# One VectorE product for the weighted one-hots of all parts or heads, and the attention product two sets later

## What is computed

```python
def spmm(x):
    msgs = edge_val[:, None] * x[edge_col]
    return jax.ops.segment_sum(msgs, edge_row, num_segments=n)
acc = cur = ebds
for _ in range(3):
    cur = spmm(cur)
    acc = acc + cur
x = _layernorm(x + acc)
...
h = (x @ W_node.T).reshape(num_nodes, 4, 32)
att = leaky(sum([h[src], h[tgt], e] * a, axis=-1))       # one number per edge and head
ex = exp(att - m[tgt])                                    # m: the target's maximum, at least 0
w = ex / denom[tgt]
h_prime = segment_sum(w[:, :, None] * h[src], tgt)
x = _layernorm(x + h_prime)
```

## Time and profile before

| | us |
|---|---|
| median of three runs | 1680.29 |
| profiled execution | 1682.1 |
| its span, first to last instruction | 1680.3 |
| setup, 0 to 84 | 84 |
| adjacency stage, 84 to 452 | 368 |
| three products with the matrix, 452 to 893 | 441 |
| scores, 893 to 1075 | 182 |
| attention stage, 1075 to 1650, and its end | 605 |

### The profile page before, as it was taken

How to read it: one execution, slowest core, us unless ns; L and a number is a source line. 1 busy time by engine, 2 the same in 40 slices (tenths; PEclk the granted TensorE clock), 3 DMA queues, 4 the chain that set the end, 5 groups by cost and what they waited for, 6 DMA issues and landing times.

```text
span 1680.3 us, 50213 instructions
## 1 busy us (share of the span) xinstructions
PE 1396.0 (83%) x22245; PEld 1008.0 (60%) x22245; DVE 1059.3 (63%) x2069; ACT 680.2 (40%) x1575; POOL 140.0 (8%) x102
## 2 busy tenths in 40 slices
PE   4969899986399999999997998567888886888885
PEld 4968789876344454454446888545555554555554
DVE  5499999999500010000116888788888887888873
ACT  3246565654200000001111000166766777677775
POOL 2611101110000000000000000111111011110000
PEclk9999898998799999999997999768888887788887
DMA  5628677755498879969972776200000000000000
GB/s 198 219 94 243 184 212 204 221 145 132 128 348 317 302 282 339 305 213 370 301 257 78 206 217 205 60 11 12 12 11 10 12 12 11 12 9 13 25 3 23
DMA packets 214644, 250.32 MB, mean 149 GB/s; under 512 B 43578, under 2 KB 146487, under 8 KB 214294
## 3 DMA queue, kind: packets, MB, share of 16 engines
q1 hardware_dynamic: 210422, 236.52, 43.6%
q0 software_dynamic: 4000, 10.54, 2.1%
HBM read 197.88 MB, written 49.14 MB: 147 GB/s over the span
## 4 chain that ended last, share of the span: by engine, by line
PE 47%; DVE 31%; DMA 6%; issue 5%; DVEq 4%; ACT 4%; SPq 1%; ACTq 1%; POOL 0%; POOLq 0%
PE bank L680 24%; PE bank L746 9%; PE bank L757 8%; DVE Hw L1163 8%; DVE L L1153 6%; DVE Hx L1346 5%; DVE Lq L1339 4%; DMA lob<-slp 2%; DVE sel L1278 2%; PE bank L717 2%; DMA drow<-in_dst,rowi 2%; DMA hib<-slp 2%; ACT Att L1009 1%; DVEq L1157 1%; DVE Hh L1155 1%
## 5 line engine op out<-in xcount | busy, mean ns | idle before, releaser
L1009 ACT COPY Att<-bank 128x400 f32<-128x400 f32 x800 | 334.9, 540 | 168.2 <-PE bank L746 167.5
L746 PE MATMUL bank<-Hx,Lq 64*128 64x100 f16 x6400 | 241.3, 223 | 88.9 <-DVE Hx L1346 83.3
L746 PEld LDWEIGHTS bank<-Hx,Lq 64*128 64x128 f16 x6400 | 176.6, 102 | 176.3 <-DVE Hx L1346 90.4
L757 PE MATMUL bank<-Att,xa 128*32 128x128 f32 x5000 | 243.0, 307 | 37.8 <-ACT oT L1016 37.8
L607 PE MATMUL bank<-L,Hw 128*52 128x128 bf16 x4800 | 178.1, 233 | 56.2 <-DVE Hw L1163 53.8
L1346 DVE TENSOR_TENSOR Hx<-Hq,wdup 128x832 f16<-128x832 f16 x400 | 205.3, 588 | 4.1 <-issue 0.4
L607 PEld LDWEIGHTS bank<-L,Hw 128*52 128x52 bf16 x4800 | 154.1, 113 | 65.4 <-DVE Hw L1163 58.7
L1163 DVE TENSOR_TENSOR Hw<-Hh,dup 64x832 bf16<-64x832 bf16 x300 | 176.0, 587 | 8.1 <-PE bank L607 1.1
L889 ACT COPY rows<-bank 116x512 f32<-116x512 f32 x200 | 117.2, 586 | 151.2 <-PE bank L607 142.4
L757 PEld LDWEIGHTS bank<-Att,xa 128*32 128x32 f32 x5000 | 123.8, 117 | 77.5 <-ACT Att L1009 41.6
L717 PE MATMUL bank<-Tp,lob 128*128 128x100 bf16 x2418 | 152.5, 210 | 15.6 <-DVE sel L1278 13.6
(11 more groups left out here) (174 smaller groups left out, 1362.8 us busy)
## 6 DMA issues: line engine op xcount, KB each, us to landing
pieces<-adj SPq DMA_DIRECT2D x90, 1280.0 KB, 8.9
adj<-rows SPq DMA_DIRECT2D x100, 416.0 KB
lob<-slp SPq DMA_DIRECT2D x26, 992.0 KB, 6.2
ea<-in_edge_attr SPq DMA_DIRECT2D x25, 992.0 KB, 8.1
hib<-slp SPq DMA_DIRECT2D x78, 64.0 KB, 4.8
pieces<-adj SPq DMA_DIRECT2D x15, 320.0 KB, 3.1
lh_d<-dup SPq DMA_DIRECT2D x25, 64.0 KB, 3.9
lhd<-lh_d SPq DMA_DIRECT2D x25, 64.0 KB, 1.8
```

What stands on the lines that cost most here:

```text
L746: m = pe.matmul(bank[i % 3 * 2 + d][:, v * H * NB:(v + 1) * H * NB].rearrange("p (h i) -> p h i", h=H), Lq[n % 2][rows, pp, :], Hx[n % 2][ ...
L757: m = pe.matmul(bank[7][h * HD:(h + 1) * HD, 0:P], xa[:, i, h * HD:(h + 1) * HD], Att[j % 2][:, h * NB + i, :], start=(i == 0), stop=(i == ...
L1009: m = act.copy(o[:, d, :, :], bank[i % 3 * 2 + d][:, 0:4 * H * NB].rearrange("p (q i) -> p i q", q=4))
```

## The change

The weights of a slot are laid beside each other, and one product covers them all.

- Adjacency: `dup` keeps the low and the high index; the three weight parts go into a new tile `dupw` in which a slot's parts stand beside each other. TensorE's `turn_records` writes them into the bank three words apart for that, and ScalarE's `duplicate` becomes two copies. `Hw` has the part inside the slot. `Hh` is made once for both halves, in the first. The six products become two, one for each half of the partitions, of 96 x 26 elements.
- Attention: the same with `wdup`, where a slot's four heads stand beside each other (`turn_weights` writes four words apart), with `Hq` made once for both halves, and with two products of 3328 elements instead of eight of 832.
- The attention product of the block before starts behind set 2 (`LATE`) and is spread over 14 sets instead of 16. The turn of the result comes behind set 1 instead of set 2. ScalarE copies `oT` ahead of set 0's evacuation instead of behind it.

```diff
+LATE = 2
...
-                Hw = [sb(f"Hw{i}", [P, 3, HP, 2, HIP], BF16, c) for i in range(2)]
-                Hh = sb("Hh", [P, 2, HP, HIP], BF16, c)
+                Hw = [sb(f"Hw{i}", [P, HP, 3, 2, HIP], BF16, c) for i in range(2)]
+                Hh = sb("Hh", [P, 2, U, HIP], BF16, c)
...
-                dup = sb("dup", [P, 3, 5, U, 2], BF16, c)
+                dup, dupw = sb("dup", [P, 3, 2, U, 2], BF16, c), sb("dupw", [P, 3, U, 3, 2], BF16, c)
...
-            wdup = sb("wdup", [P, 2, 2 * H, U, 2], F16, c)
+            wdup = sb("wdup", [P, 2, 2, U, H, 2], F16, c)
...
                 for q in range(5):
-                    m = pe.matmul(bank[2][:, q * U:(q + 1) * U], Z[:, j % 2, q, :], Jb[:, :], start=True, stop=True)
+                    o = bank[2][:, q * U:(q + 1) * U] if q < 2 else bank[2][:, 2 * U:5 * U].rearrange("p (u k) -> p u k", k=3)[:, :, q - 2]
+                    m = pe.matmul(o, Z[:, j % 2, q, :], Jb[:, :], start=True, stop=True)
...
                 for q in range(2 * H):
-                    m = pe.matmul(bank[6][:, q * U:(q + 1) * U], Z16[:, j % 2, q // H, q % H, :], J16[:, :], start=True, stop=True)
+                    m = pe.matmul(bank[6][:, :].rearrange("p (k u h) -> p k u h", k=2, h=H)[:, q // H, :, q % H],
+                                  Z16[:, j % 2, q // H, q % H, :], J16[:, :], start=True, stop=True)
...
-                        if 1 <= j <= NB:
-                            product(j - 1, q * NB // SETS, (q + 1) * NB // SETS)
-                        if q == 2 and j >= 2:
+                        if 1 <= j <= NB and q >= LATE:
+                            product(j - 1, (q - LATE) * NB // (SETS - LATE), (q - LATE + 1) * NB // (SETS - LATE))
+                        if q == 1 and j >= 2:
                             turn_result(j - 2)
...
                 act.copy(dup[:, j % 3, :, :, :].rearrange("p q u k -> p (q u) k"),
-                         bank[2][:, 0:5 * U].rearrange("p (n o) -> p n o", o=1).broadcast_to([P, 5 * U, 2])).then_inc(s["dup_sb"], 1)
+                         bank[2][:, 0:2 * U].rearrange("p (n o) -> p n o", o=1).broadcast_to([P, 2 * U, 2]))
+                act.copy(dupw[:, j % 3, :, :, :].rearrange("p u q k -> p (u q) k"),
+                         bank[2][:, 2 * U:5 * U].rearrange("p (n o) -> p n o", o=1).broadcast_to([P, 3 * U, 2])).then_inc(s["dup_sb"], 1)
...
+                        if q == 0 and j >= 2:
+                            result_evacuated(j - 2)
                         if j < NB:
                             weights_set(j, q)
-                        if q == 0 and j >= 2:
-                            result_evacuated(j - 2)
...
+            def beside(a, n):
+                return a.rearrange("p u (o n k) -> p u o n k", o=1, k=2).broadcast_to([a.shape[0], HP, n, HIP // 2, 2])
+            def inside(a):
+                return a.rearrange("p u q (o k) -> p u q o k", o=1).broadcast_to([a.shape[0], HP, a.shape[2], HIP // 2, 2])
...
-                dve.tensor_tensor(Hh[:, n % 2, :, :].rearrange("p u (n k) -> p u n k", k=2), pair_hi,
-                                  spread(dup[:, j % 3, 1, us, :], HIP // 2), ALU.is_equal)
+                if hf == 0:
+                    dve.tensor_tensor(Hh[:, j % 2, :, :].rearrange("p u (n k) -> p u n k", k=2), pair_hi, spread(dup[:, j % 3, 1, :, :], HIP // 2),
+                                      ALU.is_equal)
...
-                for k in range(3):
-                    for d in range(2):
-                        rows = slice(d * U, (d + 1) * U)
-                        m = dve.tensor_tensor(Hw[n % 2][rows, k, :, d, :].rearrange("p u (n k) -> p u n k", k=2),
-                                              Hh[rows, n % 2, :, :].rearrange("p u (n k) -> p u n k", k=2),
-                                              spread(dup[rows, j % 3, 2 + k, us, :], HIP // 2), ALU.mult)
+                for d in range(2):
+                    rows = slice(d * U, (d + 1) * U)
+                    m = dve.tensor_tensor(Hw[n % 2][rows, :, :, d, :].rearrange("p u q (n k) -> p u q n k", k=2),
+                                          beside(Hh[rows, j % 2, us, :], 3), inside(dupw[rows, j % 3, us, :, :]), ALU.mult)
...
-                dve.tensor_tensor(Hq[:, n % 2, :, :].rearrange("p u (n k) -> p u n k", k=2), pair_hi,
-                                  spread(lhd[:, j % 3, 1, us, :], HIP // 2), ALU.is_equal)
+                if hf == 0:
+                    dve.tensor_tensor(Hq[:, j % 2, :, :].rearrange("p u (n k) -> p u n k", k=2), pair_hi, spread(lhd[:, j % 3, 1, :, :], HIP // 2),
+                                      ALU.is_equal)
                 dve.drain()
                 for k in range(2):
-                    for h in range(H):
-                        m = dve.tensor_tensor(Hx[n % 2][:, k, :, h, :].rearrange("p u (n k) -> p u n k", k=2),
-                                              Hq[:, n % 2, :, :].rearrange("p u (n k) -> p u n k", k=2),
-                                              spread(wdup[:, j % 2, k * H + h, us, :], HIP // 2), ALU.mult)
+                    m = dve.tensor_tensor(Hx[n % 2][:, k, :, :, :].rearrange("p u h (n k) -> p u h n k", k=2),
+                                          beside(Hq[:, j % 2, us, :], H), inside(wdup[:, j % 2, k, us, :, :]), ALU.mult)
```

More of the change, by code:

```diff
@@ L167, in build @@
             Lq = [sb(f"Lq{i}", [P, HP, P], F16, c) for i in range(2)]
-            Hq = sb("Hq", [P, 2, HP, HIP], F16, c)
+            Hq = sb("Hq", [P, 2, U, HIP], F16, c)
             Hx = [sb(f"Hx{i}", [P, 2, HP, H, HIP], F16, c) for i in range(2)]
@@ L274, in store_dup @@
                 sp.wait_ge(s["dup_sb"], j + 1)
-                sp.dma_start(lh_d[j, :, :], dup[:, j % 3, 0:2, :, :].rearrange("p q u k -> p (q u k)")).then_inc(s[f"dup{j % 3}"], 16)
+                sp.dma_start(lh_d[j, :, :], dup[:, j % 3, :, :, :].rearrange("p q u k -> p (q u k)")).then_inc(s[f"dup{j % 3}"], 16)
             def adjacency():
@@ L607, in octet @@
                         mm = pe.matmul(bank[m % 2][c * U:c * U + 2 * HIP, v * P:(v + 1) * P],
-                                       Hw[n % 2][:, k, pp, :, :].rearrange("p d i -> p (d i)"), L[n % LB][:, pp, :],
+                                       Hw[n % 2][:, pp, k, :, :].rearrange("p d i -> p (d i)"), L[n % LB][:, pp, :],
                                        start=(k == 0), stop=(k == 2), tile_position=(0, c * U))
@@ L997, in duplicate_weights @@
                     act.wait_ge(s["hx_ready"], 2 * (j - 1))
-                act.copy(wdup[:, j % 2, :, :, :].rearrange("p q u k -> p (q u) k"),
+                act.copy(wdup[:, j % 2, :, :, :, :].rearrange("p q u h k -> p (q u h) k"),
                          bank[6][:, :].rearrange("p (n o) -> p n o", o=1).broadcast_to([P, BANK, 2])).then_inc(s["wdup_sb"], 1)
```

4 lines of the change are left out of this document (2 added, 2 removed).

## The result

The changed kernel takes 1602.3 us (median; 1599.3 to 1605.0), the kernel before 1680.1 in the same session. The ratio is 0.9538, with a 95% interval of 0.9523 to 0.9554: 78 us less, where 73 were forecast (1607, range 1588 to 1645). The profiled execution took 1605.0 us, its span is 1603.3. The total given for a kernel is the median of its runs, without one of experiment 8 that took 4137 us where the other three took 1605 to 1609.

The account below looks back on a forecast made before the run. VectorE was taken to bound the adjacency, and a loop through VectorE, TensorE and ScalarE the attention stage. 1682.1 - 31 (adjacency) - 42 (attention) = 1609 us, 1607 on the median's scale, range 1588 to 1645.

Parts of the forecast that it names:

- Price of the merged products: VectorE, both stages: 1.02 us for 1664 elements, 1.46 for 2496, 1.89 for 3328.
- the line: VectorE product time from products of 832 and 4096 elements: 0.522 ns an element plus 153 ns.
- The rival of one element at a time: VectorE, both stages: merged products stream at 1.044 ns an element, total near 1890 us; chance 0.06.
- the 3.5 us that I took off for TensorE: Adjacency: loss from TensorE's low-clock rounds reaching VectorE, taken from 34.5 us to leave 31 us gained.
- the low clock last from set 0 on to 5.8 us: Attention, TensorE: sets 0 to 4 and the turn of the result run slow, so set 8 starts at 9.31 us.
- TensorE late by a hair: Attention, set 8: TensorE arrives at 9.31 us, after VectorE's second-half Hx at 9.03.
- both changes are needed: Attention, set 8: with the old second half, Hx would come at 9.94 us instead of 9.03.
- the 1.76 us a round: Attention: gain from a round of 21.95 us to 20.19; 40 us in 23 rounds.
- The end of 53 us: Attention: largest gain, if TensorE is never slow and the round is VectorE's 19.18 + 0.73 us.
- Writes with a step: Turns writing into the bank 3 or 4 words apart: same time taken, 0.41 us for the weights' turn.
- the rival's price: Slow stepped writes in the turns: at double time, 0.41 us in each of 23 attention rounds, 9 us; chance 0.11.
- 1 us to the block behind the last `Lq`: Attention: gain for the last block, where one shorter half counts; part of the 42 us.

Follow-up runs that it names:

- experiment 8: Changed kernel with ScalarE's copy of oT put behind the evacuation of set 0 again, the product still starting at set 2: 1607.6 us, ratio 0.9568.
- experiment 1: Kernel before with only the adjacency part of the change (Hw in two products, Hh once a round, dupw, stepped records' turn): 1644.9 us, ratio 0.978.
- experiments 2 and 3: On the kernel before: first, only the merged products of attention, 1678.2 us; second, only the later attention product with oT copied earlier, 1662.4 us.
- Experiment 4: Changed kernel with both turns writing their columns densely again, so outputs aren't the reference's: 1604.6 us, ratio 0.954.
- experiments 9 and 10: Weights' turn and copy behind set 7, finish ahead of the odd half: on the kernel before, 1677.9 us; on the changed kernel without later product, 1640.6 us.

## Why the prediction was right, point by point

- **Price of the merged products.** 1889 and 1453 ns measured, 1.89 and 1.46 us worked out by the line; 1019 ns for 1664 elements, 1.02 worked out. The rival of one element at a time is out.
- **Adjacency.** The round is 12.75 us, 12.77 forecast. The term was mis-sized by the 3.5 us that I took off for TensorE: 34.3 us came in the trace (the first product with the matrix at 431.13, was 465.43) and 35.4 in experiment 1. VectorE waited 2.0 us for TensorE in the stage of after. The step that failed is the belief that the rounds at a low clock would come as before and hand half of their delay on. From `L` to `L`, 6 of 24 rounds of before stand at 0.74 to 0.84 (not 7, as I had counted), and of after 21 at 1.00 and three at 0.85 to 0.87. TensorE also waits less for `Hw` there, 27.4 us instead of 53.8; that this is why the clock stayed up isn't shown. And in experiment 1, where four rounds stood at 0.73 to 0.90, VectorE waited for TensorE only 3.1 us in the whole stage.
- **Attention.** 38.4 + 4.9 = 43.3 us, 42 forecast. The common round is 20.22, forecast 20.19, but by steps that miss in opposite directions. Set 8 starts at 9.09 us and not at 9.31: I had the low clock last from set 0 on to 5.8 us, with five slow sets. In the round shown it stands from 1.1 to 4.5 us behind set 0, with two sets and a part of one slow, so TensorE is ready at 8.40 and VectorE's `Hx`, at 9.03 as worked out, ends last. "TensorE late by a hair" was wrong, "both changes are needed" right (experiments 2 and 3). From set 8 to `Lq` are 4.07 us, not 3.87, and that is the turn.
- **Luck in the sum of the attention.** I took the 1.76 us a round from a round of 21.95 us, but the twelve rounds of the earlier trace rows last 22.19 in the mean. Two forms take turns in most of them: 22.00 us with set 0 at 1.2 GHz, the one that I read, and 22.43 with set 0 at 2.4 GHz. So the ordinary round fell by 2.0 us, and four long rounds gave some 5 us back; the two nearly cancel. The end of 53 us, too, comes out only from the mean of 22.19: 21.95 - 19.91 = 2.04 us in 23 rounds, and 2 us, are 49. Below stand set 0 of the round of before that I didn't read, and the `Lq` 22.43 us behind the last one in the earlier trace rows.

```profile
1295.47 0.54 PE L746 MATMUL bank<-Hx,Lq 64*128 64x100 f16 x16 [2.77 <-DVE Hx L1346]
```
```profile
1310.87 2.29 DVE L1339 TENSOR_TENSOR Lq<-iota_lo,lhd 128x4096 f16<-128x4096 bf16 x1 [2.31 <-PE bank L746]
```

- **Writes with a step.** I took no cost; 0.21 us was right, half of the rival's price. The rule of the Trainium skill ("SBUF — State Buffer", section "Door 1: The DMA port swizzle"), that an access to PSUM which isn't contiguous slows matmuls, agrees in direction: 0.62 us against 0.41. Experiment 4 shows the price in the round and not in the total.
- **What I had not foreseen** is the long form of the round: four rounds of 21.5 us, some 5 us in all. The clock entered my sum as a stretch behind set 0 only.
- **The ends of the stage.** I gave 1 us to the block behind the last `Lq`; it gave 4.9. TensorE waits 4.8 us for `oT` there (0.58 and 4.19, both ahead of the turn of the result) instead of 6.7 (1.30 and 0.67 ahead of the product, 4.76 ahead of the turn), and the clock is higher (mean 0.88 from the last `Lq` to the end, was 0.77).

So 1602 instead of 1607 is, in the trace, 3 us more of adjacency (33.8 where 31 were forecast) and 3.9 more at the end, less 2.6 in the loop of the attention (38.4 where 41 were forecast).

## What to carry to other kernels

A loop over three engines gets shorter only where the last arrival is moved: here a shorter VectorE and an earlier product brought 2 and 18 us alone and 43 together, and moving the turn that was left on the path brought 28 more. Before a step is moved ahead on an engine, look at what it waits for: here its own rows take 0.8 us, and its wait took 2.6 and 3.3 us a round in the mean (experiments 9 and 10). And where TensorE is freed to arrive earlier at a wait, put nothing that others need right behind that wait: here the turn that stood there took 1.03 us instead of 0.62 in the long rounds.
